# Attention and expert layer, batch by batch: the value products of two head pairs share one PSUM bank and one copy, with new instruction lists

## The reference

```
h  = layernorm(x) * (1 + ca) + sa
h  = rmsnorm(h) * norm_w
q, k, v = h @ Wq, h @ Wk, h @ Wv            # 16 heads of 64
a  = softmax(causal(q @ k.T / 8)) @ v       # per head, 256 x 256
a  = sigmoid(h @ Wgate) * a
x  = x + ga * (a @ Wout)                    # 1024 -> 128
h2 = layernorm(x) * (1 + cb) + sb
mlp     = (silu(h2 @ Wg + bg) * (h2 @ Wu + bu)) @ Wd + bd
experts = product keys: two sets of 64 keys for each of 4 heads, top 8 of each,
          top 8 of their 64 sums, softmax of these, and with the 512 rows of
          down_embed and up_embed: sum over k of silu(h2 . down[k]) * w[k] * up[k]
x  = x + gb * (mlp + experts)
```

## Time and profile before

| | |
|---|---|
| median of 3 runs | 1404.91 us (1401.65 to 1404.97) |
| profiled execution | 1400.69 us |
| its span | 1398.8 us |
| TensorE (PE) busy | 1369.1 us, 98% |
| ScalarE (ACT) busy | 1264.6 us, 90% |
| VectorE (DVE) busy | 1214.9 us, 87% |
| GpSimd (POOL) busy | 1080.4 us, 77% |
| share of TensorE in the chain that ended last | 93% |

### The profile page before, as it was taken

The page is one execution under the profiler, slowest core; times in us unless marked ns, Lnnn a source line. Parts: engine busy times, 40 slices in busy tenths (PEclk is TensorE's granted clock), DMA queues, the critical chain, the costliest instruction groups (busy, mean ns, idle before and its releaser), DMA issues.

```text
span 1398.8 us, 39734 instructions
## 1 busy us (share of the span) xinstructions
PE 1369.1 (98%) x11491; PEld 1157.3 (83%) x11491; DVE 1214.9 (87%) x5314; ACT 1264.6 (90%) x4212; POOL 1080.4 (77%) x1252
## 2 busy tenths in 40 slices
PE   6899999999999999999999999999999999999998
PEld 4778888888888888888888888888888888888877
DVE  6688898988898988898988898988898988898877
ACT  6889999999999999999999999999999999999975
POOL 2158888888888888888888888888888888888770
DMA  4000000000000000000000000000000000000000
GB/s 137 16 19 19 17 10 20 21 21 17 15 9 21 21 21 17 15 9 21 21 21 17 15 9 21 21 21 17 15 9 21 21 21 17 15 9 24 11 15 11
DMA packets 51042, 27.74 MB, mean 20 GB/s; under 512 B 10337, under 2 KB 50209, under 8 KB 51009
## 3 DMA queue, kind: packets, MB, share of 16 engines
q1 hardware_dynamic: 50768, 26.91, 7.3%
q10 hardware_dynamic: 240, 0.43, 0.1%
HBM read 23.02 MB, written 4.31 MB: 20 GB/s over the span
## 4 chain that ended last, share of the span: by engine, by line
PE 93%; DVE 3%; ACT 2%; issue 1%; POOL 1%; DMA 0%; SPq 0%; DVEq 0%; POOLq 0%
PE pW L1580 12%; PE pS L1648 12%; PE pW L1582 10%; PE pW L1581 10%; PE pW L1661 9%; PE pW L1689 8%; PE pS L1638 8%; PE pS L1634 7%; PE pW L1731 4%; PE pW L1734 4%; PE pW L1665 4%; PE pW L1722 2%; PE pW L1594 2%; ACT pS L693 1%; DVE pS L1126 0%
## 5 line engine op out<-in xcount | busy, mean ns | idle before, releaser
L693 ACT ACTIVATE pS<-pS,nmx 128x128 f32<-128x128 f32 (+1 forms) x1024 | 390.0, 437 | 31.3 <-DVE nmx L1126 30.7
L525 POOL TENSOR_TENSOR fexp<-fexp,fsum 128x512 f32<-128x512 f32 x240 | 316.5, 1347 | 90.6 <-DVE fexp L1277 90.6
L1126 DVE CUSTOM_DVE_ANT_0 pS<-pS,mask 128x128 f32<-128x128 f32 (+1 forms) x1024 | 332.3, 387 | 51.4 <-PE pS L1638 49.4
L516 POOL TENSOR_TENSOR fsum<-ex 128x512 f32<-128x512 f32 x248 | 251.8, 1047 | 1.3 <-ACT ex L741 1.3
L685 ACT COPY pT<-pS 128x768 f32<-128x768 f32 x256 | 206.1, 817 | 24.1 <-PE pS L1648 23.8
L1648 PE MATMUL pS<-ident,p_sb 128*128 128x128 f32 x1536 | 206.7, 274 | 6.8 <-DVE p_sb L1151 6.6
L1151 DVE TENSOR_TENSOR p_sb<-pS,coef 128x256 f32<-128x256 f32 (+2 forms) x512 | 208.9, 449 | 4.5
L693 ACT ACTIVATION_READ_ACCUMULATOR pS<-pS,nmx 128x1 f32 x1024 | 198.4, 194 | 0.0
L1648 PEld LDWEIGHTS pS<-ident,p_sb 128*128 128x128 f32 x1536 | 175.2, 141 | 27.6 <-DVE p_sb L1151 8.5
L1661 PE MATMUL pW<-pT,v 128*64 128x256 f32 x1024 | 162.3, 395 | 0.1
L1277 DVE TENSOR_SCALAR fexp<-fsum,top,rz 128x512 f32<-128x512 f32 x240 | 156.3, 702 | 0.0
(11 more groups left out here) (211 smaller groups left out, 3674.0 us busy)
## 6 DMA issues: line engine op xcount, KB each, us to landing
x_in<-in_L_attn_tokens SPq DMA_DIRECT2D x32, 128.0 KB, 2.1
x_res<-in_L_attn_tokens SPq DMA_DIRECT2D x32, 128.0 KB, 2.8
modB<-mods_dram SPq DMA_DIRECT2D x32, 128.0 KB, 2.9
modA<-mods_dram SPq DMA_DIRECT2D x31, 128.0 KB, 3.1
out<-yo SPq DMA_DIRECT2D x31, 128.0 KB, 1.9
modC<-mods_dram SPq DMA_DIRECT2D x32, 64.0 KB, 3.1
fsum<-in_L_attn_Wkv SPq DMA_DIRECT2D x1, 512.0 KB, 6.4
w_out<-in_L_attn_Wout SPq DMA_DIRECT2D x1, 512.0 KB, 7.3
```

The source lines that it names most:

```text
L516: ins = nc.gpsimd.tensor_tensor(fsum[:, k, h], ex[:, k, h, 0:NX].unsqueeze(2).broadcast_to([P, NX, NK]), ex[:, k, RH + h, :].unsqueeze(1). ...
L525: ins = nc.gpsimd.tensor_tensor(fexp[:, k, h, :], fexp[:, k, h, :], fsum[:, k, h].rearrange("p i j -> p (i j)"), ALU.mult)
L693: ins = nc.scalar.activation(ps, ps, ACT.Exp, bias=nmx[:, p % 2, h, k:k + 1], scale=-1.0, accum_out=den(p)[:, h, k:k + 1])
L1126: ins = nc.vector.tensor_tensor_reduce(out=ps, in0=ps, in1=mask[:, (1 - k) * P:2 * P], scale=-1.0, scalar=LARGEST, op0=ALU.add, op1=ALU.mi ...
```

## The change

Pairs 2m and 2m + 1 now write their value products side by side into one bank, columns 0 to 255 and 256 to 511. Only the even one waits for the bank, only the odd one reports it full, and one copy of 512 columns takes both out. Pair 0 reports to a semaphore of its own (`pT0_read`), for which copy_transposes(2) waits. The bank table has four jobs fewer, and it and the lists are dealt anew: in TensorE's main list scores and value products all come in twos. The project_out job waits for the release of PV 3. GpSimd runs add_bias and rstd1 after add_heads(0), and rms1 after add_heads(1). The opening and drain lists get the same replacement (in the opening scores(3) comes before the value products of pair 0, and those of pairs 2 and 4 move back to stand beside 3 and 5).

```diff
@@ -233,12 +234,11 @@
         y_gated = ev("y_gated", 1)
 
 
-        order = [("GU", 1, -2), ("D", 0, -2), ("V", 0, 0), ("PV", 6, -1), ("PV", 7, -1), ("V", 3, 0), ("QK", 2, 0),
-                 ("V", 4, 0), ("QK", 3, 0), ("QK", 4, 0), ("D", 1, -2), ("QK", 5, 0), ("V", 5, 0), ("GU", 2, -2),
-                 ("V", 1, 0), ("op", 0, -1), ("QK", 6, 0), ("GU", 3, -2), ("PV", 0, 0), ("PV", 1, 0), ("PV", 2, 0),
-                 ("hT", 0, -1), ("PV", 3, 0), ("QK", 7, 0), ("ET", 0, -2), ("V", 2, 0), ("sim", 0, -1),
-                 ("sim", 1, -1), ("PV", 4, 0), ("PV", 5, 0), ("xT", 0, 1), ("y", 0, -2), ("ET", 1, -2),
-                 ("GU", 0, -1), ("QK", 0, 1), ("QK", 1, 1)]
+        order = [("V", 3, 0), ("QK", 2, 0), ("QK", 3, 0), ("V", 0, 0), ("PV", 3, -1), ("GU", 1, -2), ("GU", 2, -2),
+                 ("GU", 3, -2), ("D", 0, -2), ("op", 0, -1), ("QK", 4, 0), ("V", 4, 0), ("QK", 5, 0), ("V", 1, 0),
+                 ("V", 2, 0), ("D", 1, -2), ("PV", 0, 0), ("V", 5, 0), ("hT", 0, -1), ("PV", 1, 0), ("QK", 6, 0),
+                 ("QK", 7, 0), ("sim", 0, -1), ("ET", 0, -2), ("sim", 1, -1), ("PV", 2, 0), ("xT", 0, 1),
+                 ("ET", 1, -2), ("y", 0, -2), ("GU", 0, -1), ("QK", 0, 1), ("QK", 1, 1)]
         assert len(order) % NW == 0, len(order)
         bank_of, off_of, place, count = {}, {}, {}, {}
         for n, (name, k, off) in enumerate(order):
@@ -250,15 +250,14 @@
         work_free = {key: ev(f"work_free{key[0]}_{key[1] + 2}", n) for key, n in count.items()}
 
         A, Z = B - 2, B - 1
-        drain = [("GU", 1, A, 2), ("PV", 6, Z, 3), ("PV", 7, Z, 0), ("D", 0, A, 1), ("op", 0, Z, 3), ("D", 1, A, 2), ("GU", 2, A, 0),
+        drain = [("GU", 1, A, 2), ("PV", 3, Z, 3), ("D", 0, A, 1), ("op", 0, Z, 3), ("D", 1, A, 2), ("GU", 2, A, 0),
                  ("GU", 3, A, 1), ("hT", 0, Z, 3), ("sim", 0, Z, 2), ("sim", 1, Z, 3), ("ET", 0, A, 0), ("ET", 1, A, 1), ("y", 0, A, 2),
                  ("GU", 0, Z, 0), ("GU", 1, Z, 3), ("D", 0, Z, 1), ("D", 1, Z, 3), ("GU", 2, Z, 0), ("ET", 0, Z, 1), ("GU", 3, Z, 2),
                  ("ET", 1, Z, 3), ("y", 0, Z, 0), ("y", 1, Z, 1)]
         off_of["y", 1] = off_of["y", 0]
         opening = [("xT", 0, 0, 2), ("QK", 0, 0, 2), ("QK", 1, 0, 3), ("V", 0, 0, 0), ("V", 3, 0, 3), ("QK", 2, 0, 1), ("QK", 3, 0, 2),
-                   ("V", 1, 0, 0), ("PV", 0, 0, 0), ("PV", 1, 0, 1), ("QK", 4, 0, 2), ("V", 4, 0, 1), ("QK", 5, 0, 0), ("PV", 2, 0, 3),
-                   ("V", 2, 0, 1), ("QK", 6, 0, 0), ("PV", 3, 0, 1), ("QK", 7, 0, 0), ("V", 5, 0, 3), ("PV", 4, 0, 0), ("xT", 0, 1, 2),
-                   ("PV", 5, 0, 1), ("QK", 0, 1, 2), ("QK", 1, 1, 3)]
+                   ("V", 1, 0, 0), ("PV", 0, 0, 1), ("QK", 4, 0, 2), ("V", 4, 0, 3), ("QK", 5, 0, 0), ("PV", 1, 0, 3), ("V", 2, 0, 1),
+                   ("QK", 6, 0, 0), ("QK", 7, 0, 1), ("V", 5, 0, 0), ("PV", 2, 0, 3), ("xT", 0, 1, 2), ("QK", 0, 1, 2), ("QK", 1, 1, 0)]
         opened, drained = {}, {}
         for name, k, b, n in drain:
             drained[name, k, b] = drain_full[n], drain_free[n], n, sum(1 for job in drained.values() if job[2] == n) + 1
@@ -617,15 +616,15 @@
                 products(0)
                 candidates()
                 products(1)
-                rstd1()
-                add_bias()
                 weigh(0)
                 add_heads(0)
+                add_bias()
+                rstd1()
                 fold(0)
                 rstd2()
-                rms1()
                 weigh(1)
                 add_heads(1)
+                rms1()
                 fold(1)
                 shift_top()
             run(pool, body)
@@ -674,14 +673,14 @@
 
                 def weighted(p):
                     if w.has("PV", p):
-                        evacuate(aoT[:, p, :], w.bank("PV", p)[:, 0:N], "PV", p)
+                        evacuate(aoT[:, 2 * p:2 * p + 2, :].rearrange("p j t -> p (j t)"), w.bank("PV", p)[:, :], "PV", p)
 
                 def copy_transposes(p, off):
                     if w.live(off):
                         b = i + off
                         act.wait_ge(S(t_full), at(t_full, b, p + 1))
                         if p == 2:
-                            w.wait_full("PV", 0, b)
+                            act.wait_ge(S(pT0_read), at(pT0_read, b, 1))
                         nc.scalar.copy(pT[:, p % 2], pS[:, p % 2, :, 0:SW]).then_inc(S(pT_ready), 1)
 
                 def exp_scores(p):
@@ -1649,22 +1640,27 @@
                         ins.then_inc(S(t_full), 1)
 
                 def weigh_values(p):
-                    if w.has("PV", p):
+                    if w.has("PV", p // 2):
                         if 2 * p in VCUT:
                             for k in range(TB):
                                 w.wait_released("V", k * NV + VCUT.index(2 * p))
-                        pe.wait_ge(S(pT_ready), at(pT_ready, w.batch("PV", p), p + 1))
-                        w.wait_free("PV", p)
-                        bank = w.bank("PV", p)
+                        pe.wait_ge(S(pT_ready), at(pT_ready, w.batch("PV", p // 2), p + 1))
+                        if p % 2 == 0:
+                            w.wait_free("PV", p // 2)
+                        lo, mid, hi = p % 2 * N, p % 2 * N + P, p % 2 * N + N
+                        bank = w.bank("PV", p // 2)
                         for h in range(2):
                             hd = slice((2 * p + h) * DH, (2 * p + h + 1) * DH)
-                            mm(bank[h * DH:(h + 1) * DH, 0:N], v[:, 0, hd], pT[:, p % 2, h, 0:2 * P],
+                            mm(bank[h * DH:(h + 1) * DH, lo:hi], v[:, 0, hd], pT[:, p % 2, h, 0:2 * P],
                                start=True, stop=False, skip_group_check=True)
                         for h in range(2):
                             hd = slice((2 * p + h) * DH, (2 * p + h + 1) * DH)
-                            ins = mm(bank[h * DH:(h + 1) * DH, P:N], v[:, 1, hd], pT[:, p % 2, h, 2 * P:3 * P],
+                            ins = mm(bank[h * DH:(h + 1) * DH, mid:hi], v[:, 1, hd], pT[:, p % 2, h, 2 * P:3 * P],
                                      start=False, stop=True, skip_group_check=True)
-                        w.filled(ins, "PV", p)
+                        if p % 2 == 1:
+                            w.filled(ins, "PV", p // 2)
+                        elif p == 0:
+                            ins.then_inc(S(pT0_read), 1)
 
                 def transpose_x():
                     if w.has("xT"):
@@ -1680,7 +1676,7 @@
 
                 def project_out():
                     if w.has("op"):
-                        w.wait_released("PV", NP - 1, f)
+                        w.wait_released("PV", NP // 2 - 1, f)
                         if isinstance(i, int) and i == 1:
                             pe.wait_ge(const_dve, 1)
                         w.wait_free("op")
```

More of the change, by code:

```diff
@@ L844, in body @@
                     exp_scores(5)
-                    weighted(3)
+                    weighted(1)
                     scale_head(5)
@@ L946, in body @@
-                scale_head(5)
-                copy_transposes(4, 0)
-                experts(0)
-                values(2)
-                copy_transposes(5, 0)
-                rms_scale()
-                weighted(4)
-                expert_exp(0)
-                total(1)
-                weighted(5)
+                modulate_h()
+                weighted(0)
+                values(5)
+                high_part(h2T_high, h2T, "hT")
+                exp_scores(4)
+                exp_scores(5)
@@ L1465, in body @@
                 ln1(stats1)
+                sum_top()
+                invert_top()
+                choose(0, 0)
+                choose(0, 1)
+                row_max(0)
+                row_max(1)
+                invert(0)
+                coefficients(0)
+                normalise(0)
+                invert(1)
+                coefficients(1)
+                normalise(1)
+                choose(1, 0)
                 bias_product(1)
```

174 lines of the change are left out of this document (79 added, 95 removed).

## The result

The changed kernel takes 1409.47 us (median of 12 runs, 1407.59 to 1412.03), the kernel before 1404.95 in the same comparison (12 runs, 1400.61 to 1406.40). The ratio is 1.0037 with a 95% interval of 1.0027 to 1.0047: slower by 4.5 us, more than the measurement is uncertain. The forecast was 1403 us, 2 us faster. The profiled execution took 1410.66 us, its span 1408.8 us.

What follows compares the result with a forecast made beforehand. TensorE's own queue was taken as the bound. Batches at 40.7 + 1.2 + 0.05 = 41.95 us against 41.98 give -1 us, opening and drain -1: 1400.69 becomes 1398.7, plus 4.2 for the median 1403 us; range 1385 to 1420.

Steps and rivals of the forecast that it cites:

- A list without waits takes 40.7 us: TensorE's batch: 41.98 us less 0.70 for four fewer changes of kind and 0.57 for the old real waits.
- T1 waits for scale_head(1), 0.25 us: Second score transposes of a batch: turn at 8.8, but their input scale_head(1) ends at 9.03.
- The walk: Method: the four engines' new lists stepped through by timeline distances from T7's start as zero; good to some 0.3 us a batch.
- choose(0) is hardly caught; row_max(0) 0.1 late: VectorE's first half: choose mostly escapes GpSimd's products(1), the fourth ends at 3.95, so row_max(0) starts 0.1 late.
- VectorE packed to add_residual, which would end at 18.15; modB lands beside it: From row_max(0), 14.2 us of VectorE work; modB lands at 17.25, so gate_attention waits some 0.15 us.
- TensorE 1.0 us behind at V1: At V1: QK5 waits 0.3 us for gated_down(0) and V1 0.25 to 0.4 us more, leaving TensorE 1.0 us behind.
- scores(6) 1.2 us behind, paced by ScalarE's queue with weighted(1) in it: S4 to S6: ScalarE's queue puts scores(6) 1.06 us behind a gapless list where V1 was 0.86; 1.2 us taken.
- Tail free: Batch's end: x transposes wait 0.05 us for rms_scale; T6 and T7 have 1 us of slack.
- Period 41.95: Time per batch: 40.7 + 1.2 + 0.05 us against 41.98, giving -1 us over thirty batches.
- Opening and drain, -1 us: Kernel's two ends: value products slip into TensorE's waits for copies, -2 to +2 us, taken as -1.
- Small waits, 1387: Rival, chance 0.28: new waits only 0.4 to 0.9 us a batch, period 41.1 to 41.6, some 1387 us.
- VectorE sets the end through choose(0): Rival, chance 0.30: choose(0) caught by products(1) delays row_max(0) through to V1; 1416 us at 0.4 more, 1431 at 0.9.

Runs made afterwards that it cites:

- e8: Changed kernel with project_down(0) between the first score transposes, ScalarE's copies of pairs 0 and 4 earlier, add_bias, rms_scale and project_ffn(0) moved: 1551.24 us, ratio 1.1025.
- e4: Changed kernel with ScalarE's copy_transposes(0) ahead of gate_up(1) and copy_transposes(4), (5) ahead of queries(7): 1410.87 us, ratio 1.0036 to the kernel before.
- e13: Changed kernel with VectorE's choose cut to 64 of 512 columns in bodies 3 to 30: 1422.99 us, ratio 1.0129 to the kernel before.
- e14: Changed kernel with ScalarE's copy of the value products cut from 512 to 64 columns in bodies 3 to 30: 1409.66 us, ratio 1.0028 to the kernel before.
- e9: Changed kernel with GpSimd's add_bias behind the products in the first drain body instead of first: 1407.89 us, ratio 1.0022 to the kernel before.
- e5: Kernel before's main lists with the merged bank, the single copy and the change's opening and drain lists: 1402.12 us, ratio 0.9979 to the kernel before.
- e6: Changed kernel's main lists with a bank and copy for each pair and the old opening and drain lists: 1430.27 us, ratio 1.0176 to the kernel before.
- e17: e13 with VectorE's shift1 and square1 moved right behind choose(1, 1): 1401.46 us, ratio 0.9961 to the kernel before.

## Why the prediction was wrong, step by step

- *A list without waits takes 40.7 us:* nearly 0.4 too short. In medians of the steps from one job's start to the next one's, T1's wait costs 0.37 us of the changed kernel's 42.05, V1's 0.39 (the step from QK5 to it is 1.10 us, in e8 0.71) and scores(6)'s 0.22 (e4 takes it away); 41.1 us are left. The four changes of kind gave 0.59 us and not 0.70: scores(4) and (5), their value products and the h transposes take 3.27 us for 3.69, scores(6) and (7) and theirs 3.00 for 3.17.
- *T1 waits for scale_head(1), 0.25 us:* right in kind, measured 0.37 to 0.39. The walk took choose(0) as part of the cause; e13 shows that it is not.
- *choose(0) is hardly caught; row_max(0) 0.1 late:* right (row_max(0) at 4.04 on the walk's clock, forecast 3.95).
- *VectorE packed to add_residual, which would end at 18.15; modB lands beside it:* right, 18.19, and modB's wait is in the rows. (The terms for modB add up to 17.1, not to the 17.25 that the forecast gives; that gate_attention did start at 17.25 is a coincidence.)
- *TensorE 1.0 us behind at V1:* laid end to end by the steps of the chain of which the earlier trace rows shows a part (an estimate), the new list has T2 at 19.12; it comes at 20.10, 0.98 us behind. That the two agree is luck in part: the 0.3 us of QK5 isn't there, V1's wait costs 0.39 (0.25 to 0.4 forecast), T1's 0.37 instead of 0.25, and the other 0.2 is in steps longer than the sum has them.
- *scores(6) 1.2 us behind, paced by ScalarE's queue with weighted(1) in it:* measured 1.43 (31.95 against 30.52 end to end, the same estimate), and the mechanism fell in part: e14 shows that the copies of value products have no share in it; e4 shows 0.2 us for the place of the copy of T4 behind queries(7).
- *Tail free:* right for the change. That it is free only as long as V1's wait stands was not seen: the walk priced the lock for choose alone and passed over shift1.
- *Period 41.95:* measured 42.03 to 42.07, 0.1 us more a batch, some 3 us in thirty. Two errors partly cancel here: the list without waits is nearly 0.4 us longer, and the waits are 1.0 us and not 1.25.
- *Opening and drain, -1 us:* this is the step that failed. The end is 2.7 us longer. The forecast looked at waits for copies there and not at what a later finish does to add_bias at the head of GpSimd's drain list. The last add_residual is 2.7 us late behind an add_bias that is 2.8 late; e9 takes 1.7 us of it back and loses the rest to modB, and e5 and e6 show that it comes with the main lists and not with the drain list. What the opening adds stays open (between nothing and 1.9 us).
- *Small waits, 1387:* didn't come; the waits are 1.0 us a batch, above the 0.9 at which that rival ends. *VectorE sets the end through choose(0):* didn't come; the loss has other places.

With these sizes the forecast's own sum comes out: 1403, plus 3 for the period and 3.7 for the ends (2.7 in place of -1, with nothing for the opening), is 1409.7. The change holds two edits of opposite sign: the shared bank and single copy, which gain 3 us (e5, interval 1.3 to 4.5 us), and the new main lists of all engines, which lose 7 to 8.

## What to carry to other kernels

Before taking a wait away, list what starts earlier for it, and look for VectorE instructions with two SBUF inputs or in a two-port mode that then fall on a GpSimd instruction: a wait of 0.3 us can be what keeps a meeting of 0.9 us away. Where two edits come together, time each alone; here one was worth keeping. A later last step of the batch can be free in the loop and be paid once in the drain, where the next body's first instruction waits for it (2.7 us here).

## What the runs showed of the hardware

- Cutting VectorE's work by some 1.5 us a batch made the kernel 13 us slower (e13), through one instruction that grew from 0.56 to 1.44 us.
- A choose of 64 columns beside weigh took nearly as long as one of 512: 1.85 us for two (e13) and 1.96 us for two (the change). In this meeting it is the length of GpSimd's instruction (1.3 us each) that sets the pace, hardly that of VectorE's.
- shift1, a sum of 128x256 elements from two SBUF inputs, took 418 ns free of GpSimd (e17), 565 ns on the tail of an add_heads (the change) and 1445 ns when it started just after one (e13). No wait is put beside the longer one in the timeline; only its duration shows it.
- The granted clock of TensorE fell to the lower level for 3.4 us twice in the opening and once in the drain of the changed kernel, near idle stretches of 1.6 to 2.2 us, and not at all in the profiled execution of the kernel before, which has such stretches too. In e8 it fell near each of 29 waits of 2.9 us. The mean clock of the other runs (0.994 to 0.999) goes with their time, as told above; that this is what spreads the runs of one kernel over 5 us is read from that, and was not tried.
